# Two attention layers on one core: where a step's other piece of TensorE work stands among its four score matmuls

## The reference, cut to what matters

```
q, k = rope(rms(x @ wq.T)), rope(rms(x @ wk.T))        # layer 0; layer 1 adds biases instead
scores = einsum('bhtd,bhsd->bhts', q, k) * scale        # 512 x 512 for each head
attn = softmax(scores, axis=-1)
y = einsum('bhts,bhsd->bhtd', attn, v)
out = y.reshape(B, T, C) @ wproj.T
```

## Time and profile before

| | us |
|---|---|
| median of 3 executions | 2005.58 |
| the profiled execution, its own time | 2005.26 |
| its span in the trace | 2003.6 |
| steady part of the attention of layer 0 | about 150 to 500 |
| steady part of the attention of layer 1 | about 1283 to 1640 |

### The profile page before, as it was taken

One profiled execution on the slowest core, in us unless ns is written; L12 is line 12 of the kernel. 1 busy time (PEld: TensorE's weight loads), 2 busy tenths in 40 slices (PEclk: granted clock), 3 DMA queues, 4 the chain that ended last, 5 costly groups with the idle time before them and its releaser, 6 DMA issues. The chain is left out here.

```text
span 2003.6 us, 29490 instructions
## 1 busy us (share of the span) xinstructions
PE 1815.8 (91%) x10344; PEld 754.1 (38%) x10344; DVE 1313.3 (66%) x2598; ACT 1150.8 (57%) x1553; POOL 660.1 (33%) x918
## 2 busy tenths in 40 slices
PE   4789999998979999999999997899999996699998
PEld 3323333332224444444444443233333222355554
DVE  5488888888743544535535533788888883767674
ACT  4268878876743433324324332587778776566674
POOL 5667677762120000000000022243333311354542
PEclk8689999999989999999999998899999997799999
DMA  3345544444261000000001003333333303433420
GB/s 117 64 92 122 135 122 121 107 110 114 80 232 69 22 22 1 22 11 11 22 1 48 11 21 64 64 64 75 74 75 64 64 12 115 135 126 96 146 64 32
DMA packets 119619, 147.63 MB, mean 74 GB/s; under 512 B 19779, under 2 KB 102838, under 8 KB 117430
## 3 DMA queue, kind: packets, MB, share of 16 engines
q1 hardware_dynamic: 119478, 145.79, 27.5%
HBM read 100.34 MB, written 45.14 MB: 73 GB/s over the span
## 5 line engine op out<-in xcount | busy, mean ns | idle before, releaser
L853 DVE TENSOR_REDUCE A_M<-A_SM 128x1 f16<-128x512 f32 x1024 | 654.2, 684 | 133.1 <-PE A_SM L1068 130.7
L624 ACT ACTIVATE A_P<-A_ST 128x1024 f32<-128x1024 f32 x512 | 524.0, 1026 | 162.3 <-PE A_ST L1084 155.4
L1068 PE MATMUL A_SM<-A_KT,A_QS 48*128 48x512 f16 x1024 | 351.9, 395 | 47.7 <-DVE A_M L853 39.8
L1619 PE MATMUL B_PA<-B_Hh,B_wh 128*128 128x512 f16 x1024 | 388.1, 379 | 3.1 <-DVE B_Hl L1584 3.1
L1619 PE MATMUL B_PA<-B_Hl,B_wh 128*128 128x512 f16 x1024 | 388.1, 379 | 0.0
L1538 ACT ACTIVATE B_af<-B_PA,B_sv 128x512 f32<-128x512 f32 x192 | 132.0, 688 | 357.1 <-PE B_PA L1619 356.9
L1084 PE MATMUL A_ST<-A_QS,A_KT 49*128 49x512 f16 x1024 | 297.5, 383 | 2.2 <-DMA A_QS<-A_rows 1.7
L1101 PE MATMUL A_AV<-A_P,A_V 128*32 128x512 f32 x2048 | 272.8, 605 | 4.2 <-ACT A_P L624 3.6
L1068 PEld LDWEIGHTS A_SM<-A_KT,A_QS 48*128 48x128 f16 x1024 | 83.5, 93 | 431.7 <-DVE A_M L853 383.9
L1582 DVE TENSOR_SCALAR B_Hh<-B_af 128x512 f16<-128x512 f32 x128 | 62.8, 491 | 278.7 <-ACT B_af L1538 278.7
L1333 POOL TENSOR_TENSOR B_hl<-B_hf,B_hh 128x512 f16<-128x512 f32 x14 | 16.2, 1156 | 506.4 <-ACT B_hh L1349 506.4
(11 more groups left out here) (362 smaller groups left out, 3223.4 us busy)
## 6 DMA issues: line engine op xcount, KB each, us to landing
D_w_st<-in_we_dram SPq DMA_DIRECT2D x16, 1024.0 KB, 5.0
qk<-A_tr SPq DMA_DIRECT2D x58, 256.0 KB, 2.5
A_KT<-qk SPq DMA_DIRECT2D x96, 128.0 KB, 5.0
A_QS<-qk SPq DMA_DIRECT2D x96, 128.0 KB, 4.6
A_w_st<-in_w_ffn_dram SPq DMA_DIRECT2D x32, 352.0 KB, 3.4
A_QS<-A_rows SPq DMA_DIRECT2D x512, 0.5 KB
w_hi<-A_f_hi SPq DMA_DIRECT2D x32, 176.0 KB, 3.5
w_lo<-A_f_lo SPq DMA_DIRECT2D x32, 176.0 KB, 3.6
```

The source lines that it names most:

```text
L624: nc.scalar.activation(P[:, st, 2 * pair:2 * pair + 2, :], ST[:, u % 2, :, :], ACT.Exp, scale=1.0 / math.sqrt(HD)).then_inc(exp_s, 1)
L853: nc.vector.tensor_reduce(M[G % 2][:, o:o + 1], SM[:, n % 2, :], AX, ALU.max, negate=True).then_inc(max_s, 1)
L1068: nc.tensor.matmul(SM[:, n % 2, :], QS[b % 2][r, 2 * g + pair, tt * 128:tt * 128 + 128], KT[b % 2][r, 2 * g + pair, :], start=True, stop=T ...
L1619: ins = nc.tensor.matmul(out, a, c, start=start and kt == 0 and n_ == 0, stop=stop and kt == kts[-1] and n_ == len(ops) - 1)
```

## The change

In a step of TensorE the second pair (`scores(p, 0)` and the odd raw tile) moves from ahead of the piece to behind it. The transposes of step 1 stay last. No instruction is added or removed, and no other engine's list changes.

```
                 raw(2 * p + AHEAD)
                 if 0 <= p < PAIRS * B:
                     scores(p, 1)
-                    scores(p, 0)
-                raw(2 * p + AHEAD + 1)
                 name, n = jobs.get(p, ("", 0))
                 if name:
                     job(name, n, (0, 1) if len(slots_of(name, n)) == 1 else (1,))
...
                     if G is not None:
                         values(G, st)
+                if 0 <= p < PAIRS * B:
+                    scores(p, 0)
+                raw(2 * p + AHEAD + 1)
                 G = group_at(p, 9)
                 if G is not None:
                     pe.wait_ge(y_cp, G + 1)
```

## The result

The changed kernel took 2196.65 us (median of 4, from 2189.22 to 2199.94), the kernel before 2005.65 us beside it. The ratio is 1.095, with a 95% interval from 1.0917 to 1.0982. The direction was forecast; the forecast of 2141 us was 56 us low, and the end of the range, 2195, is 2 us under the median.

The account below looks back on a forecast made before the run. The prediction took the attention to run at the speed of TensorE's list, with little waiting. 16 x 1.8 + 16 x 2.3 + 32 x 2.2 = 136 us, added to 2005.26, gave 2141 us, range 2085 to 2195.

Parts of the forecast that it names:

- The exp that `values` wait for: Main term: in steps 6 and 0, `values` wait for the exp of the step just ahead; 0.94 us in step 6.
- the chart of one group: Start times worked out from step 5 to step 2, layer 1, empty step 7; step 2 begins 2.0 us later.
- the sign of 80: Sign expected in the profile after: waits of `values` for exp come to 80 us or more in total.
- Behind step 2, some comes back, ... I take back 0.2: Layer 1, behind step 2: raw tiles find their maxima long taken, so 0.2 us per group is taken off.
- the sum had 1.8 and 2.3: Layer 1, time added per group: 1.8 us with an empty step 7, 2.3 with a projection there, 16 groups each.
- I take 2.2 us for 32 groups; bounds are 1.5 and 3.: Layer 0: each of 32 groups gets 2.2 us longer, with bounds of 1.5 and 3 us per group.
- small work: Layer 0: ScalarE has more small work there, which puts some exps back further; within the 2.2 us per group.
- So the same pattern runs one tile shifted. I take 0.: Raw tiles and maxima: each raw tile still waits for the maximum two tiles back; 0 us, ends -40 and +40.
- The turn of the mode: Step 1, pair between job and transposes: at most 0.2 us per group; 0 in the sum, 13 us in the range.
- So I expect it to stay: Granted clock: expected to stay at 1.00 despite TensorE's new waits, as a window with 8.21 of 10 busy did.
- The rival with the falling clock: Rival, 5%: a tenth of 671 busy us at half the clock would add 67 us, giving 2208 us.
- The rival that was faster: Rival, 4%: the piece fills raw matmuls' waits for maxima, whose 39.8 us go, giving 1965 us.

## Why the forecast was right in kind and too low

**Where the sum comes from.** With the raw tiles placed as in the changed kernel, and the second score product put ahead step by step, medians form a chain: 2197 with none ahead, 2170 with steps 5 and 7, 2137 with 0, 2098 with 2 and 4, 2072 with all, and 2005 in the kernel before.

| what stands behind the piece | forecast | measured in the chain |
|---|---|---|
| scores in steps 5, 7 and 0 | 136 together | 27 + 33 |
| scores in steps 2 and 4 | 0 | 39 |
| scores in steps 1, 3 and 6 | 0 | 26 |
| odd raw tiles, all steps, every exp early | 0, ends -40 and +40 | 67 |

The chain depends on its order, since the costs overlap, and its versions break pairs of matmuls which the changed kernel keeps (16 us of busy time in the second, the lone raw tile of step 1 in the last but one). So it shows that a term isn't nothing, and not the share that each has in the changed kernel; that is better read from the waits of the table in the first section. Put behind one at a time in the kernel before, steps 5, 7 and 0 cost 37, 22 and 45 us, each with the price of three raw tiles in a row in it.

**The exp that `values` wait for.** The mechanism was right, and so was the chart of one group up to the transposes, to 0.1 us; with an empty step 7, the wait of 0.5 us in step 0 that it put down to exp was one for maxima. Between first and last exp, TensorE's idle time at the two places grew by 108 us, where the forecast's 136 hold some time besides. `values` alone come to 77.7 us, a little under the sign of 80. What the chart did not say is that these waits are only the last ones of a queue: freeing steps 5 and 7 alone gave 27 us.

**"Behind step 2, some comes back, ... I take back 0.2" is the step that failed first.** It looked only at raw tiles and their maxima. Nothing is seen to come back; the job of step 2 lost up to 0.60 us on its bank, and the jobs' waits for a bank in layer 1 rose from 3.2 to 11.6 us. Layer 1 grew by 9.9 us per 32 steps, 2.5 per group, where the sum had 1.8 and 2.3. That is some 14 us over 32 groups.

**Layer 0: "I take 2.2 us for 32 groups; bounds are 1.5 and 3."** It measured 110 / 32 = 3.4, over its own upper bound, some 40 us more than forecast. The term named "small work" on ScalarE, and not what empties the bank: an instruction behind exp in ScalarE's list, or behind the odd maximum in VectorE's. Full projections in steps 2 and 4 with transposes in step 3 made it 1.87 and 1.20 us of waiting. Over the whole of layer 0, though, waits for banks rose by 17 us (10.5 to 27.7), those for maxima by 16 (14.5 to 30.6), and 45 us more passed at the low clock, an estimated 14 us by the price below. The waits for exp and copy themselves grew by 55, where the sum had 70.

**"So the same pattern runs one tile shifted. I take 0."** The pattern of raw tiles on TensorE is the same, but the time was not: the raw matmuls wait 22 us more for maxima in the changed kernel. That is a term that the sum lacked, within its ends of 40. Alone, the move cost 67 us, over the upper end, but more than half of that is busy time, a part of which only that version has. VectorE's and ScalarE's lists were not shifted with TensorE's, so the odd tile is late relative to what those lists have behind it; for the banks this is seen in the rows. Why the maxima are waited for more often in layer 0 of that run (84 times against 29) stays open.

**The turn of the mode, costed at nothing.** With the whole pair between job and transposes step 1 took 0.26 us longer, near the 0.2 at most; with a raw tile alone, that has lost its partner, 0.46. Whether it costs something in the changed kernel stays open: the run that took it away moved exp of step 1 too. The Trainium skill, "TensorEngine Tiling (Array Packing)", Key Properties, says that a change of the tiling mode drains TensorE; the 0.95 us against 0.49 agree with it in kind.

**The clock.** "So I expect it to stay" was partly wrong. From first to last exp of both layers, the granted clock stood at its low level for 72.9 us, against 11.0 before. What such a stretch costs can be read from two sequences of layer 0 in the changed kernel that have nearly the same number of instructions on every engine (columns as in the earlier trace rows):

```profile
257.00:329.50 72.50, 56.25 (x384) 18.62 (x380) 52.88 (x100) 47.58 (x66) 43.17 (x54) 1.00 0.40 100
329.50:404.00 74.50, 58.67 (x386) 18.96 (x384) 52.64 (x99) 47.58 (x66) 43.19 (x54) 0.95 0.39 91
```

The second has 6.8 us at the low clock and is 2.2 us longer from exp to exp (74.4 against 72.2), 0.32 us for each. At that price the 62 us more are an estimated 20 us. The rival with the falling clock, 5% and 67 us more, came in smaller size beside the forecast's own mechanism, which the chances had as alternatives. The forecast's 56 us of error are 16 us in layer 1 (81.4 against 65.6) and 40 in layer 0 (110 against 70.4), clock included.

**The steps that failed** are the terms at nothing or below: waits of jobs for their bank, which no term named (26 us more), raw matmuls waiting for maxima (22 us more), the take-back behind step 2 (13 us that did not come), and the clock (an estimated 20 us). They come to more than the 56 us of error, because the waits that the main term was about grew by 108 us and not by 136; how far the two can be set against one another is rough, as the split of TensorE's time is.

**The rival that was faster** had it that the waits of raw matmuls for maxima go. They rose from 39.8 to 62.6 us.

## What to carry to other kernels

When a producer is moved behind other work in one engine's list, follow every list that is in fixed order behind it, and not only the instructions that wait for it by name. Here, buffers that another engine empties behind the late instruction cost 26 us, and no term of the forecast had them. Where several late results form a queue on one engine, putting back only the last of them returns little. In an experiment that puts back single steps, the change of order between neighbours has a cost of its own. A version that keeps one of the two moved parts uniform avoids that, but count the matmuls that lose their partner. And where such a run lands on its forecast, look whether the wait that was forecast is there: twice here it was another one.

## What the runs showed of the hardware

The clock fell more often than the prediction had it. The changed kernel with the pair behind the transposes shows it most. Two windows of its layer 0 and three of layer 1:

```profile
200.00:300.00 100.00, 73.27 (x460) 22.28 (x458) 63.06 (x117) 56.93 (x78) 52.03 (x64) 0.91 0.36 88
300.00:400.00 100.00, 73.57 (x482) 23.93 (x480) 64.60 (x126) 60.77 (x85) 53.74 (x68) 0.95 0.30 76
1480.00:1580.00 100.00, 78.37 (x461) 21.29 (x458) 62.45 (x121) 56.39 (x66) 29.11 (x59) 0.86 0.21 43
1600.00:1700.00 100.00, 76.24 (x509) 23.08 (x501) 66.25 (x124) 60.06 (x72) 27.95 (x56) 0.97 0.34 63
1700.00:1800.00 100.00, 74.78 (x502) 21.56 (x501) 67.36 (x128) 63.17 (x76) 31.11 (x64) 1.00 0.22 49
```

TensorE is busy for 73 to 78% there, with no stop longer than 1.9 us. In the first four windows the granted clock falls to 1.2 GHz for 7 to 27 us each, and for 230 us in all within the two attentions. In the last it stays at 1.00, with 75% busy and stops of up to 1.6 us. So neither the busy share nor the longest stop tells these windows apart, and what decides stays open. The Trainium skill, "TensorE: Matmul & The Clock Gate", section on psum-queue depth-cycling, tells of a clock that swings because TensorE idles briefly and often. This run agrees with it in kind: the clock swings, and the stops are many and short. That they are the cause is not shown; filling one of them in the changed kernel did not help. The prediction set one window with 8.21 of 10 us busy, at 1.00, against that rule. In the changed kernel the window of layer 0 above with 56.25 of 72.5 us busy stays at 1.00 as well, and the next one, with 58.67 of 74.5, is at 0.95.
